# A self-attention state transposed in its own step, with new orders for the ramp, the end and the stacked rows

## What is computed

```python
x = x + tanh(g_xattn) * cross_attention(layernorm(x), ctx)        # 16 heads of 8
z = layernorm(x)
h = rms(z) * n1
q, k, v = rms(heads(h @ wq.T)), rms(heads(h @ wk.T)), heads(h @ wv.T)
z = z + causal_attention(q, k, v) @ wo.T                          # first 32 channels unchanged
f = rms(z) * n2
moe = sum over 4 experts of gate_e(f) * expert_e(f)               # top 2 of 4, gelu and silu layers
x = x + tanh(g_ffn) * (z + moe)                                   # moe's first 32 channels are zero
```

## Time and profile before

| what | value |
|---|---|
| median of three runs | 1121.92 us (1121.64 to 1123.22) |
| the profiled execution's own time | 1120.12 us |
| its span, first to last instruction | 1118.4 us |
| granted TensorE clock, share of full speed | 0.982 |
| TensorE busy (matmuls) | 1010.6 us, 90% |
| VectorE busy | 806.0 us, 72% |
| ScalarE busy | 734.0 us, 66% |
| GpSimd busy | 334.9 us, 30% |
| hardware DMA queue of SP | 111.54 MB, 38.2% of 16 engines' span |

### The profile page before, as it was taken

How to read it: one execution, slowest core, us unless ns; L and a number is a source line. 1 busy time by engine, 2 the same in 40 slices (tenths; PEclk the granted TensorE clock), 3 DMA queues, 4 the chain that set the end, 5 groups by cost and what they waited for, 6 DMA issues and landing times.

```text
span 1118.4 us, 25981 instructions
## 1 busy us (share of the span) xinstructions
PE 1010.6 (90%) x8578; PEld 622.6 (56%) x8578; DVE 806.0 (72%) x2170; ACT 734.0 (66%) x1331; POOL 334.9 (30%) x458
## 2 busy tenths in 40 slices
PE   3657799999999999999999999999999999998897
PEld 1334456656565655656565565655565565555454
DVE  7457777777877777787778777787777778655423
ACT  3455667676776766677676667768676767765453
POOL 6422314051422414151331405142241415132120
PEclk9979899999999999999999999999999999999899
DMA  6426533454433334454333344443333444403100
GB/s 193 111 48 185 142 94 71 117 126 123 126 104 98 101 85 111 123 126 123 100 102 87 87 122 126 123 121 102 97 92 89 125 123 112 118 9 93 33 10 10
DMA packets 77156, 114.26 MB, mean 102 GB/s; under 512 B 7616, under 2 KB 40000, under 8 KB 76992
## 3 DMA queue, kind: packets, MB, share of 16 engines
q1 hardware_dynamic: 76752, 111.54, 38.2%
q10 hardware_dynamic: 368, 2.24, 0.6%
HBM read 58.97 MB, written 53.74 MB: 101 GB/s over the span
## 4 chain that ended last, share of the span: by engine, by line
PE 56%; DVE 23%; ACT 10%; issue 8%; DMA 2%; POOL 0%; DVEq 0%; SPq 0%; ACTq 0%; POOLq 0%
PE ps_pv L1161 9%; PE ps_w L1187 7%; PE ps_s2a L1140 6%; PE ps_s2a L1198 5%; PE ps_s2b L1140 4%; PE ps_s2b L1205 4%; ACT probs L787 4%; DVE mpadB L915 4%; PE ps_t L1044 4%; DVE mpadA L915 3%; PE ps_w L1205 3%; PE ps_t L1174 2%; PE ps_w L1122 2%; PE ps_w L1118 2%; DVE ym L944 2%
## 5 line engine op out<-in xcount | busy, mean ns | idle before, releaser
L787 ACT ACTIVATE probs<-ps_s2a 120x512 f32<-120x512 f32 (+1 forms) x256 | 153.7, 600 | 92.3 <-PE ps_s2a L1140 86.8
L915 DVE TENSOR_REDUCE mpadB<-ps_w 128x4 f32<-128x512 f32 x256 | 158.6, 682 | 29.0 <-PE ps_w L1122 29.0
L915 DVE TENSOR_REDUCE mpadA<-ps_w 128x4 f32<-128x480 f32 x252 | 147.8, 649 | 36.7 <-PE ps_w L1122 36.6
L787 ACT ACTIVATE probs<-ps_s2b 120x512 f32<-120x512 f32 (+1 forms) x256 | 154.0, 602 | 0.0
L678 POOL TENSOR_SCALAR_AFFINE_SELECT probs<-probs 128x1024 f32<-128x1024 f32 x128 | 139.8, 1092 | 0.1
L1187 PE MATMUL ps_w<-W,hid 128*128 128x96 f32 x1024 | 130.0, 281 | 4.4 <-DVE split_k L821 1.1
L1187 PEld LDWEIGHTS ps_w<-W,hid 128*128 128x128 f32 x1024 | 122.2, 195 | 16.4 <-issue 13.5
L649 POOL TENSOR_TENSOR rB<-vrB,neg_half 128x4 f32<-128x4 f32 x16 | 16.1, 1007 | 374.1 <-DVE veB L814 374.1
L1140 PE MATMUL ps_s2a<-qdA,kstA 128*120 128x512 f32 x128 | 69.3, 541 | 14.9 <-issue 7.9
L944 DVE SCALAR_TENSOR_TENSOR ym<-ps_w,gates,ym 128x96 f32<-128x96 f32 x192 | 47.6, 310 | 43.6 <-PE ps_w L1187 43.5
L1198 PE MATMUL ps_s2a<-hid,W 128*128 128x512 f32 x160 | 78.4, 604 | 0.0
...
## 6 DMA issues: line engine op xcount, KB each, us to landing
...
```

Of the source, the lines that this page charges most:

```text
L787: nc.scalar.activation(probs[0:k, slot_of(part, *index), :], bank[0:k, :], ACT.Exp, scale=SCALE if part == "A" else 1.0).then_inc(done, 1)
L915: nc.vector.tensor_reduce(mneg[OP[part]][:, :, c, b], bank[:, 0:HT * k].rearrange("p (h k) -> p h k", h=HT), AX.X, ALU.max, negate=True).t ...
```

## The change

The use hT moves from part B at a step's start to part A near its end, between e0_up chunk 0 and chunk 1. GpSimd's base moves to the end of the step, and outside the first group waits for the block-diagonal keys kd of its step. B's first qk product waits for all w banks of the step before, in place of the hT bank. The loads of x and ctx become two uses, and in the ramp both run a step ahead. The stacks' rows are interleaved: head slot j goes into the rows j, j + 4, j + 8 and so on, 24 of 96, and the maxima into row 96. The second, third and fourth ramp steps and all end steps have orders of their own. In the fourth, B's work of the start of the list and A's estimates stand in new places, then the list goes on as in SCHEDULE. In the last steps the order of the uses and some rings differ (the new orders of steps 17 and 18 are not shown).

```diff
 def self_attention():
-    return (one("N", "load", 0, None) + exact("D", 0, 0) + one("B", "hT") + down(1) + exact("D", 0, 2)
+    return (one("N", "load", 0, None) + one("N", "ctx", 0, None) + exact("D", 0, 0) + down(1) + exact("D", 0, 2)
             + one("B", "qk", 0) + one("B", "qk", 1) + one("B", "qk", 2) + one("B", "qk", 3)
             + exact("D", 1, 0) + estimate("A", 0) + exact("D", 1, 2)
...
-            + one("N", "base", 0, None) + fill("D", "e2_l1", 1) + fill("D", "e3_down", 0) + one("D", "gates", 1, None)
+            + fill("D", "e2_l1", 1) + fill("D", "e3_down", 0) + one("D", "gates", 1, None)
             + one("B", "mT") + one("N", "q") + one("D", "gates", 2, None) + one("A", "norm", 0, None) + one("N", "v") + one("N", "k")
-            + fill("D", "e0_up", 0) + fill("D", "e0_up", 1, "w") + one("D", "gates", 3, None))
+            + fill("D", "e0_up", 0) + one("A", "hT") + fill("D", "e0_up", 1, "w") + one("D", "gates", 3, None)
+            + one("N", "base", 0, None))
...
 def first_group():
-    return (one("N", "load", 0, None) + one("N", "stats", 0, None) + one("N", "norm", 0, None) + one("N", "base", 0, None)
+    return (one("N", "stats", 0, None) + one("N", "norm", 0, None) + one("N", "base", 0, None) + one("N", "load", 0, None)
             + one("N", "xT") + one("N", "q", 0, "f") + one("N", "k", 0, "f") + one("N", "v", 0, "pv")
-            + estimate("A", 0) + estimate("A", 1, "ffww") + estimate("A", 2, "wwff") + estimate("A", 3) + one("A", "mT"))
+            + estimate("A", 0) + estimate("A", 1, "ffww") + estimate("A", 2, "wwff") + estimate("A", 3) + one("A", "mT")
+            + one("N", "ctx", 0, None))
 def second_group():
...
+    return (one("N", "stats", 0, None) + one("N", "norm", 0, None)
+            + exact("A", 0, 0) + exact("A", 0, 2) + one("N", "xT") + exact("A", 1, 0) + one("N", "q") + exact("A", 1, 2) + one("N", "k")
+            + values("A", 0) + exact("A", 2, 0) + estimate("A", 0) + exact("A", 2, 2) + values("A", 1)
+            + exact("A", 3, 0) + one("A", "oT", 0, "t") + estimate("A", 1) + exact("A", 3, 2) + values("A", 2)
+            + one("A", "nT", 0, "t") + estimate("A", 2) + values("A", 3) + one("A", "oT", 1) + one("A", "wo", 0, "t") + one("N", "v")
+            + one("A", "nT", 1, "t") + estimate("A", 3) + one("A", "wo", 1, "t") + one("A", "stats", 0, None)
+            + one("A", "mT") + one("A", "norm", 0, None) + one("A", "hT")
+            + one("N", "base", 0, None) + one("N", "ctx", 0, None) + one("N", "load", 0, None))
 def third_group():
...
+    return (exact("A", 0, 0) + exact("A", 0, 2) + exact("A", 1, 0) + exact("A", 1, 2) + values("A", 0)
+            + one("B", "qk", 0) + one("B", "qk", 1) + one("B", "qk", 2) + one("B", "qk", 3)
+            + exact("A", 2, 0) + one("B", "squares", 0, None) + exact("A", 2, 2) + values("A", 1)
+            + exact("A", 3, 0) + one("A", "oT", 0, "t") + exact("A", 3, 2) + one("B", "sums", 0, None) + one("B", "root", 0, None)
+            + values("A", 2) + one("B", "init", 0, None) + one("B", "copy", 0, None) + one("A", "nT", 0, "t") + one("B", "scale", 0, None)
+            + values("A", 3) + one("A", "wo", 0, "t") + one("N", "stats", 0, None) + one("A", "oT", 1) + one("B", "v")
+            + one("B", "qT") + one("B", "kT") + one("N", "norm", 0, None) + one("A", "nT", 1, "t")
+            + estimate("B", 0) + one("A", "wo", 1, "t") + one("N", "xT") + estimate("B", 1) + one("N", "q") + estimate("B", 2)
+            + one("N", "k") + estimate("B", 3) + one("A", "stats", 0, None) + one("N", "v")
+            + one("B", "mT") + one("A", "norm", 0, None) + one("A", "hT") + one("N", "base", 0, None))
+def fourth_group():
+    return (one("N", "load", 0, None) + one("N", "ctx", 0, None) + exact("D", 0, 0) + exact("D", 0, 2)
+            + one("B", "qk", 0) + one("B", "qk", 1) + one("B", "qk", 2) + one("B", "qk", 3) + estimate("A", 0)
+            + exact("D", 1, 0) + exact("D", 1, 2) + estimate("A", 1) + one("B", "squares", 0, None) + values("D", 0)
+            + exact("D", 2, 0) + exact("D", 2, 2) + estimate("A", 2) + values("D", 1) + one("B", "sums", 0, None)
+            + exact("D", 3, 0) + one("D", "oT", 0, "t") + exact("D", 3, 2) + estimate("A", 3) + values("D", 2)
+            + one("D", "nT", 0, "t") + one("B", "root", 0, None) + one("A", "mT") + values("D", 3) + one("D", "wo", 0, "t")
+            + one("B", "scale", 0, None) + one("D", "oT", 1) + one("N", "stats", 0, None) + one("B", "qT") + one("B", "kT")
+            + one("D", "nT", 1, "t") + one("N", "norm", 0, None) + one("D", "wo", 1, "t") + one("D", "out", 0, None)
+            + one("D", "squares", 0, None)
+            + [use for use in cross_attention() + first_experts() if use[0] in "NABD"])
+def last_queries():
+    order = of_parts("ABDM")
+    late = estimate("B", 3) + one("B", "mT")
+    order = [use for use in order if use not in late]
+    at = order.index(("D", "fill", ("e1_w1", 1), "f"))
+    order = order[:at] + estimate("B", 3) + order[at:]
+    at = order.index(("D", "fill", ("e2_l1", 1), "f"))
+    return order[:at] + one("B", "mT") + order[at:]
+def last_self_keys():
+    return (exact("D", 0, 0) + down(1) + exact("D", 0, 2)
+            + one("B", "qk", 0) + one("B", "qk", 1) + one("B", "qk", 2) + one("B", "qk", 3)
+            + exact("D", 1, 0) + exact("D", 1, 2) + one("B", "squares", 0, None) + values("D", 0) + exact("D", 2, 0)
+            + one("B", "sums", 0, None) + exact("D", 2, 2) + one("B", "root", 0, None) + values("D", 1) + one("B", "scale", 0, None) + down(0)
+            + exact("D", 3, 0) + one("D", "oT", 0, "t") + exact("D", 3, 2) + one("B", "qT") + one("B", "kT")
+            + values("D", 2) + one("D", "nT", 0, "t")
+            + fill("M", "e2_l2", 0) + one("D", "wo", 0, "t") + estimate("B", 0) + fill("M", "e2_l2", 1)
+            + values("D", 3) + fill("M", "e3_up", 0) + one("D", "oT", 1, "t") + estimate("B", 1) + fill("M", "e3_up", 1)
+            + one("D", "nT", 1, "t") + fill("M", "e2_l3", 0) + one("D", "wo", 1, "t") + one("D", "out", 0, None) + estimate("B", 2)
+            + fill("M", "e2_l3", 1) + estimate("B", 3) + one("D", "squares", 0, None) + down(2)
+            + one("D", "norm", 0, None) + one("B", "init", 0, None) + one("B", "copy", 0, None) + one("B", "mT")
+            + down(3) + one("M", "store", 0, None) + one("D", "xfT") + one("B", "v") + one("D", "logits")
+            + fill("D", "e1_w1", 0, "w") + fill("D", "e1_w2", 0, "w") + fill("D", "e1_w1", 1, "w") + fill("D", "e1_w2", 1, "w")
+            + fill("D", "e2_l1", 0) + fill("D", "e2_l1", 1) + fill("D", "e3_down", 0, "w")
+            + fill("D", "e0_up", 0, "w") + fill("D", "e0_up", 1, "w")
+            + one("D", "gates", 0, None) + one("D", "gates", 1, None) + one("D", "gates", 2, None) + one("D", "gates", 3, None))
...
 def banks_of(order):
-    own = [use for use in SCHEDULE if use in order] != order
+    own = any(use not in SCHEDULE for use in order)
     return bank_of_each_use(order if own else SCHEDULE)
-AHEAD = {"s1": (-1, 0), "mT": (-1, 0)}
-RAMP = [(-1, "N", first_group()), (0, "NA", second_group()), (1, "NAB", third_group()), (2, "NABD", of_parts("NABD"))]
+AHEAD = {("A", "s1"): (-1, 0), ("A", "mT"): (-1, 0), ("N", "load"): (-1, 0), ("N", "ctx"): (-1, 0)}
+RAMP = [(-1, "N", first_group()), (0, "NA", second_group()), (1, "NAB", third_group()), (2, "NABD", fourth_group())]
 LOOP = (3, NG - 1)
-TAIL = [(NG - 1, "ABDM", of_parts("ABDM")), (NG, "BDM", of_parts("BDM")), (NG + 1, "DM", last_self_values()), (NG + 2, "M", last_experts())]
+TAIL = [(NG - 1, "ABDM", last_queries()), (NG, "BDM", last_self_keys()), (NG + 1, "DM", last_self_values()), (NG + 2, "M", last_experts())]
...
-        ahead = self.parts != PARTS and part == "A" and self.t in AHEAD.get(work, ())
+        ahead = self.parts != PARTS and self.t in AHEAD.get((part, work), ())
...
-        M_ROW = HD * SPLIT
+        M_ROW = HD * SPLIT * HT
...
+            def load_x(g):
+                sp.dma_start(xt[:], x[bass.ds(g * G, G), :, :].rearrange("b t d -> t b d")).then_inc(x_loaded, 16)
+            def load_ctx(g):
+                sp.dma_start(ctT[:], ctxT[:, bass.ds(g * CT, CT)]).then_inc(ctx_loaded, 16)
...
-                        at = slice(32 * j, 32 * j + rows)
+                        at = slice(j, M_ROW, HT)
                         of = scratch[to + o].rearrange("(c j r) t -> j r c t", j=HT, r=rows)[j]
                         to_tile = qd[to][at, j, :, :] if o == "q" else kst[to][at, :, :]
...
-                        if not st.first("N"):
-                            sp.wait_ge(xn_ready, g)
-                            sp.wait_ge(x1_base, g)
-                        sp.dma_start(xt[:], x[bass.ds(g * G, G), :, :].rearrange("b t d -> t b d")).then_inc(x_loaded, 16)
-                        if not st.first("N"):
-                            sp.wait_ge(kd_ready["A"], g)
-                        if st.parts != PARTS and not st.first("N"):
```

(27 more changed lines are left out.)

47 lines of the change are left out of this document (15 added, 32 removed).

## The result

The changed kernel takes **1158.49 us** (median of four runs, 1153.97 to 1160.28) against 1122.33 of the kernel before on the same chip: ratio 1.0316, 95% interval 1.0285 to 1.0346. I had forecast 1134 with 0.60 on slower: the direction is right, and by the loop's slower steps as forecast; the size is not, and the time lies outside the range.

A forecast was written before the change was run, and what follows sets the result against it. TensorE bounds the kernel, busy 800.0 of 835.7 us in the middle steps. Seams +24.1, clock -1.0, ramp -4.5, step 15 +3.7, step 16 -9, steps 17 and 18 -1.5: +11.8 on 1121.92, given as 1134; range 1107 to 1146.

The forecast's parts named there:

- Seam, steps 1 to 3: Loop step's end: hb 0.90 us earlier, hT stalls 1.74, late gelu, exponentials, mask and copy delay ym; +1.85 per seam.
- the rival without it: Seam: the mask chain does not end last, so a seam costs only 0.7 us; total 1118, chance 0.14.
- the one without a wait at hT: Seam: hb ends before the last gelu layer's first product does, so a seam costs 0.1 us; total 1111, chance 0.18.
- Behind the seam all engines shift together: Loop: after each seam nothing was seen that gives its added 1.85 us back.
- The clock of the first loop step: The loop step of 66.17 us held lower clock; half of its extra 2.06 goes, -1.0 (0 to -2.1).
- The rival of a lower clock in all seams: Loop: the clock falls at the longer seams, 12 × 2.06 us on top; total 1158, chance 0.06.
- The ramp: Steps before the loop: earlier first scores not carried on, third step pays back first two's gain; -4.5 us (0 to -12).
- Fourth ramp step: Ramp: the 3.57 us wait before nT goes, and 0.9 of the 1.40 before the second cross scores; -4.5.
- First scores: Start of the ramp: they can start at 30.53 instead of 34.59, 4.06 us earlier, if the loads are done.
- Step 15: Behind the loop: maxima leave earlier but hT has the same seam; +3.7 us (0 to +4.5).
- Step 16: End: new order puts experts between B's estimates, cutting idle time and half clock; -9 us (0 to -15).
- Steps 17 and 18: End: 5.2 us idle in the first, mostly the unshortened chain from out to xfT; -1.5 us (0 to -5).

The follow-up runs named there:

- kept_first: The changed kernel with GpSimd's kept copy moved to the step's start, ahead of the first mask: 1137.4 us, ratio 1.0138.
- base_only: The kernel before with only GpSimd's base moved to the step's end, behind kd: 1120.93 us, ratio 0.9990.
- third_old: The changed kernel with the kernel before's order of the third ramp step, hT set at its end: 1146.06 us, ratio 1.0217.
- third_old_banks: third_old with the bank rule of the kernel before as well: 1143.72 us.
- ht_back: The changed kernel with hT put back in its old place in all steps: 1139.0 us, ratio 1.0150.
- fourth_old: The changed kernel with the loop's own order, cut to four parts, in the fourth ramp step: 1157.56 us (two runs).
- base_kept: The kernel before with base moved to the step's end behind kd and the kept copy ahead of the first mask: 1105.85 us, ratio 0.9865.
- values_back: The changed kernel with the kernel before's order of step 17: 1154.44 us.

## Why the prediction was wrong

- **Seam, steps 1 to 3: right.** Line 1010 falls to 0.17, the stall at hT is 1.67 (forecast 1.74), the fourth qk product waits 1.09 (about 1), the step grows by 1.75 (1.85). kept_first shows that the mask chain was last, so the rival without it fell, and so did the one without a wait at hT. What I had not seen is that base, moved, has a price where the exponentials are early: with hT in the next step it stands ahead of the mask, and base_only gives nothing for that. "Behind the seam all engines shift together" held; nothing gave it back.
- **The clock of the first loop step:** -2.1 instead of -1.0, and +1.3 elsewhere. The rival of a lower clock in all seams did not come: one step of twelve. That its 1158 is the time measured is chance.
- **The ramp is the step that failed.** "I carry **none** of it to the loop (0 to −4.1)" and "−4.5": measured are -3.2 before the third step and +14.8 in it. The mechanism was named ("puts the qk products behind eight score products", "strings B's four estimates on VectorE at its end"), but not priced: I let it cost what the first steps won and gave it no bound. The rows price it: +6.5 for the late qk products, +3.3 for estimates that use all four w banks and so cannot overlap N's products in those banks, +5.0 for the end, where the maxima, moved past SP's loads, wait for them to issue; the last two hold the lower clock's 4.5. third_old brings back 11.3 of the 14.8, and the 3.5 left are busy time at a lower clock; third_old_banks, at the clock of the kernel before, is 0.8 above it. hT now ends that step. With the new order this costs nothing (ht_back, without it there, takes 51.34); with the old one no run tried it alone.
- **Fourth ramp step: wrong.** The two waits did go, but three of like size took their place (5.6 for 5.0); fourth_old shows no gain. I named no wait that would be late next.
- **First scores: near, and by the mechanism forecast.** They come at 31.46 against 30.53 forecast. Their last wait is for the maxima's DMA, which was issued at 28.45 instead of 27.80 and landed at 31.37, 2.92 us later instead of 2.73. The profile names a stack load as the releaser, but the trace's landing times have the last of those at 30.88 (in the kernel before 32.88, and the maxima at 34.50):

```profile
28.45 0.55 ACTq L826 DMA_DIRECT2D qdA<-mTA  x1
...
31.46 0.75 PE L1198 MATMUL ps_s2a<-qdA,kstA 128*120 128x512 f32 x1 [3.35 <-DMA kstA<-scratch_Ak]
```

The estimate by the Trainium skill ("SBUF — State Buffer", section "Door 1: The DMA port swizzle"), that the loads are done before 27.8 since all ports are reached, did not come out. The last of them was issued only from 26.28 to 27.04 and landed at 30.88; the rate was 209 GB/s from 20.4 to 31.4, against 177 from 20.4 to 31.5 in the kernel before. The 162 of the earlier trace rows, which agreed with six ports, is no test of it, since the x load ran in that stretch too.

- **Step 15:** +2.4 instead of +3.7, inside its bounds. **Step 16: right**, -7.9 for -9 (4.6 busy time at a higher clock, 0.97 against 0.89, and 3.3 idle time), and -10.6 in base_kept's family (60.80 to 50.21).
- **Steps 17 and 18: wrong.** +5.2 for "**−1.5** (0 to −5)": values_back gives 5.1 of it back, half of it idle time and half the clock. I costed them as a gain without reading their new order against its waits; the bound allowed no loss.

The terms that failed, the ramp's (+16.5, with its seam) and step 17's (+6.7), make the whole miss of 22.0; the others together are -1.2. The median lies 4.5 above the profiled execution, at granted clocks of 0.959 to 0.967 in the other three runs against 0.968; the run at 0.967 took 1158.63, so the clock alone does not tell it.
